# A graph network in one kernel: the build loop on TensorE rotated by half a pair, and the wide comparison on VectorE cut from 128 to 126 columns

## The reference, cut to what matters

```python
x = layernorm(x + L0(x, edges))            # h = x + segment_sum(x[src], dst); MLP; residual
x = layernorm(x + L1(x, src, dst))         # two rounds: h + mean over incoming edges, MLP, relu
x = layernorm(x + L2(x, edges, weight))    # 4 steps: neigh = segment_sum(norm * h[src], dst), tanh
x = layernorm(x + L3(x, edges, attr))      # relu(segment_sum(x[src] @ W + b + attr @ We + be, dst))
```

## Time and profile before

| | |
|---|---|
| median of 3 runs | 1121.02 us (1120.48 to 1122.2) |
| the profiled execution | 1121.91 us |
| its span, first to last instruction | 1120.1 us |
| mean granted TensorE clock | 0.977 |
| build stage on TensorE | 77.0 to 271.9 us |

### The profile page before, as it was taken

One profiled execution on the slowest core, in us unless ns is written; L12 is line 12 of the kernel. 1 busy time (PEld: TensorE's weight loads), 2 busy tenths in 40 slices (PEclk: granted clock), 3 DMA queues, 4 the chain that ended last, 5 costly groups with the idle time before them and its releaser, 6 DMA issues.

```text
span 1120.1 us, 25031 instructions
## 1 busy us (share of the span) xinstructions
PE 1027.4 (92%) x10501; PEld 626.3 (56%) x10501; DVE 520.1 (46%) x945; ACT 284.9 (25%) x584; POOL 53.9 (5%) x73
## 2 busy tenths in 40 slices
PE   0246999998999999999999999999999999999997
PEld 0245877777755555455466455564455744457455
DVE  7487999994633356322323222332222334344333
ACT  0366999997500000010000000000000001112100
POOL 4500000001000000000000000000000000000000
PEclk9966999999999999999999999999999999999999
DMA  8214778788985856877569776598774987655931
GB/s 249 74 3 174 312 315 337 321 342 330 391 368 209 336 229 244 324 295 300 200 234 408 297 294 245 178 410 325 283 265 159 393 327 306 239 199 209 411 128 33
DMA packets 55910, 299.54 MB, mean 267 GB/s; under 512 B 7264, under 2 KB 10738, under 8 KB 52403
## 3 DMA queue, kind: packets, MB, share of 16 engines
q1 hardware_dynamic: 50352, 288.14, 66.5%
q0 software_dynamic: 3344, 9.67, 2.6%
q10 hardware_dynamic: 2160, 0.98, 0.4%
HBM read 235.93 MB, written 62.86 MB: 267 GB/s over the span
## 4 chain that ended last, share of the span: by engine, by line
PE 85%; ACT 6%; issue 4%; DVE 2%; DMA 2%; PEld 0%; ACTq 0%; SPq 0%; DVEq 0%; PEldq 0%
PE ps L1367 47%; PE ps L1360 18%; PE ps L1446 6%; PE ps L1470 5%; PE ps L1322 4%; PE ps L1277 2%; ACT arena L1102 2%; ACT arena L1103 2%; PE ps L1335 2%; DMA x_buf<-in_x 1%; PE ps L1209 1%; PE ps L1304 1%; ACT arena L1044 0%; PE ps L1266 0%; DMA arena<-in_dst_blocks,win_ati 0%
## 5 line engine op out<-in xcount | busy, mean ns | idle before, releaser
L1367 PE MATMUL ps<-arena 125*128 125x500 f32 (+2 forms) x700 | 267.5, 537 | 0.0
L1367 PE MATMUL ps<-arena,parts_even 125*128 125x500 f32 (+2 forms) x700 | 267.5, 537 | 0.0
L1367 PEld LDWEIGHTS ps<-arena,parts_even 125*128 125x128 f32 x700 | 129.4, 188 | 120.6 <-issue 106.7
L1367 PEld LDWEIGHTS ps<-arena 125*128 125x128 f32 x700 | 129.3, 188 | 120.5 <-issue 106.7
L1081 ACT ACTIVATE XT<-ps 128x500 f32<-128x500 f32 (+2 forms) x49 | 26.5, 540 | 491.9 <-PE ps L1335 491.9
L1360 PE MATMUL ps<-arena 125*128 125x500 f16 (+3 forms) x700 | 139.0, 352 | 1.6 <-DVE arena L761 1.3
L1102 ACT ACTIVATE arena<-ps 128x450 f16<-128x450 f32 (+1 forms) x187 | 119.4, 639 | 23.5 <-PE ps L1470 23.5
L1470 PE MATMUL ps<-arena 64*128 64x52 f16 (+1 forms) x6300 | 99.3, 179 | 24.4 <-issue 10.2
L1103 ACT ACTIVATE arena<-ps 128x450 f32<-128x450 f32 (+1 forms) x187 | 112.9, 604 | 0.0
L1470 PEld LDWEIGHTS ps<-arena 64*128 64x128 f16 x6300 | 89.4, 94 | 42.0 <-issue 21.2
L848 DVE TENSOR_TENSOR arena<-ps,dinv 125x512 f32<-125x512 f32 (+2 forms) x28 | 17.8, 634 | 202.6 <-PE ps L1322 202.6
(11 more groups left out here) (192 smaller groups left out, 738.9 us busy)
## 6 DMA issues: line engine op xcount, KB each, us to landing
arena<-weight_mats SPq DMA_DIRECT2D x20, 3250.0 KB, 11.1
arena<-weight_mats SPq DMA_DIRECT2D x20, 3000.0 KB, 10.6
arena<-count_mats SPq DMA_DIRECT2D x15, 3125.0 KB, 14.7
weight_mats<-arena SPq DMA_DIRECT2D x25, 1562.5 KB, 8.5
count_mats<-arena SPq DMA_DIRECT2D x25, 781.2 KB, 4.3
arena<-weight_mats SPq DMA_DIRECT2D x4, 2437.5 KB, 9.2
arena<-weight_mats SPq DMA_DIRECT2D x4, 2250.0 KB, 8.5
arena<-count_mats SPq DMA_DIRECT2D x3, 2343.8 KB, 9.5
```

Source lines behind the costliest of these rows:

```text
L1367: ins = t.matmul(o, xs[:, k, :], rhs, start=(k == 0), stop=(k == NC - 1))
```

## The change

Three edits.

TensorE's pair is cut into two chunks of code. The loop now runs over q from 0 to 12; its body is the odd chunk of pair q (units 8 to 14) and then, under a condition q < 12, the even chunk of pair q+1 (units 0 to 7). The separate code of pair 0 is gone, and so pair 0 runs with the lumps of units 8, 10 and 13, whose sums nobody takes; `agg0_done` starts one lower to make up for the signal that they raise. The waits for `parts0_ok` and `blank_ok` stand ahead of pair 0. At the first tile of each odd chunk there is one more wait for `hots_ok`, of a step that was already waited for.

VectorE's comparison for `hot_hi` writes columns 0 to 125 of each tile. Columns 126 and 127 are zeroed once by Pool, in three memsets ahead of the large one, and VectorE waits for them once (`edges_ok`) ahead of its first step.

```diff
+HI = NP + 1
             def fast():
                 pool.wait_ge(rec_ok, RECS)
+                for hot in hot_hi:
+                    ins = nc.gpsimd.memset(hot[:, :, HI:128], 0.0)
+                ins.then_inc(edges_ok, 1)
                 nc.gpsimd.memset(stg_c[0][:, 0], 0.0).then_inc(blank_ok, 1)
...
-                v.tensor_tensor(hot_hi[u][:, e, :].rearrange("p t (a j) -> p t a j", j=2), numbers(iota_hi, n, 128),
-                                code(hi_c[:, bass.ds(q, 1), t0:t0 + n, :], 128), ALU.is_equal)
+                v.tensor_tensor(hot_hi[u][:, e, 0:HI].rearrange("p t (a j) -> p t a j", j=2), numbers(iota_hi[:, 0:HI], n, HI),
+                                code(hi_c[:, bass.ds(q, 1), t0:t0 + n, :], HI), ALU.is_equal)
...
                 dve.wait_ge(iotas, 1)
+                dve.wait_ge(edges_ok, 1)
...
-                pe.sem_inc(agg0_done, 2)
+                pe.sem_inc(agg0_done, 1)
...
-                def pair(q, counts):
-                    for u in range(NO_UNITS if counts is None else 0, UNITS):
+                def chunk(q, odd):
+                    counts = (stg_all[0:NP, bass.ds((q + 1) % 2, 1), 0:STG_C // 2].bitcast(F16)
+                              .rearrange("p a (j k t) -> p (a j) k t", j=2, k=NC))
+                    for u in range(UNITS_OF[0], UNITS) if odd else range(0, UNITS_OF[0]):
...
-                            if T == STEP_AT[step] or counts is None and T == TPC:
+                            if T == STEP_AT[step] or T == TPC:
                                 pe.wait_ge(hots_ok, STEPS * q + step + 1)
...
-                pair(0, None)
                 pe.wait_ge(parts0_ok, 1)
                 pe.wait_ge(blank_ok, 1)
-                with pe.Fori(1, PAIRS) as q:
-                    pair(q, stg_all[0:NP, bass.ds((q + 1) % 2, 1), 0:STG_C // 2].bitcast(F16)
-                         .rearrange("p a (j k t) -> p (a j) k t", j=2, k=NC))
+                with pe.Fori(0, PAIRS) as q:
+                    chunk(q, 1)
+                    with pe.If(q < PAIRS - 1):
+                        chunk(q + 1, 0)
```

More of the change, by code:

```diff
@@ L314, in build_program @@
         iotas = sem("iotas")
+        edges_ok = sem("edges_ok")
         dve_chain = sem("dve_chain")
@@ L1450, in sum_counts @@
                             ins.then_inc(agg0_done, 1)
-                def pair(q, counts):
-                    for u in range(NO_UNITS if counts is None else 0, UNITS):
[L1454 to L1459, removed]
+                def chunk(q, odd):
+                    counts = (stg_all[0:NP, bass.ds((q + 1) % 2, 1), 0:STG_C // 2].bitcast(F16)
+                              .rearrange("p a (j k t) -> p (a j) k t", j=2, k=NC))
+                    for u in range(UNITS_OF[0], UNITS) if odd else range(0, UNITS_OF[0]):
+                        if u == LUMP_AT[0]:
+                            pe.wait_ge(counts_out, UNITS * q)
+                        if u in LUMP_AT:
+                            k0 = KCH * LUMP_AT.index(u)
+                            sum_counts(q - 1, counts, range(k0, k0 + KCH))
                         pe.wait_ge(weights_out, UNITS * q + u - SLOTS3 + 1 + OUT_PAD)
```

## The result

| | before | changed |
|---|---|---|
| median of 19 runs each, side by side | 1122.20 us | 1118.06 us |
| lowest and highest | 1119.77, 1123.79 | 1114.03, 1121.41 |
| profiled execution (span) | 1121.91 (1120.1) | 1114.69 (1112.9) |
| ratio, with its 95% interval | | 0.9969, 0.9957 to 0.9981 |

The changed kernel is faster by 0.31% by the ratio, some 3.5 us; the two medians lie 4.1 us apart. Its runs spread over 7.4 us, where those of before spread over 4.0, and the profiled execution is one of the quickest: it shows 7.2 us less of span. So this trace shows what the change can bring, and the median tells that most runs bring less.

A forecast was written before the change was run, and what follows sets the result against it. In the build, the TensorE and ScalarE ring, 14.17 us a pair, ends last, with VectorE's 14.14 beside it. Start -5.6, turn +4.6, comparison -0.1 sum to -1.1 us: 1119.9 from a median of 1121.02, range 1115.3 to 1124.0.

The forecast's parts named there:

- its first term: Start of the build, up to unit 3's lump of pair 2: 1.9 us lost, then 7.5 gained, 5.6 us earlier.
- its second: Loop turn now between units 7 and 8, where TensorE has no gap: 0.42 us a pair, 11 pairs, 4.6 us lost.
- The first rival: The turn is cheap, 0.1 to 0.25 us, or a clock fall drops out: -3.5 us, 1115.5 to 1117.5; chance 0.28.
- with both -5.5: Within the cheap-turn rival: cheap turn and one fall of the clock dropping out together give -5.5 us.
- the bound of 2.6: Start of the build: if the longer stop lets the clock fall, three lumps cost 1 us more each, only 2.6 gained.
- the last stop at 462: TensorE's stop for code at matmul 462, its block asked for inside pair 0's store burst: about 2.2 us, resuming about 97.9.
- one at 339 matmuls: TensorE's stop for code at matmul 339, in unit 1 before the store burst: about 1.2 us.
- the term of 0.215 us: At the turn, the added unconditional branch at the conditional's end costs TensorE 0.215 us, the median branch duration.
- VectorE's comparison, -0.1: L724 on 5292 elements, 0.045 us less each; only the build's first steps pass it on, 0.1 us gained.
- A loss of the packed rate: VectorE's comparison drops out of its packed rate: 37 x 2.8 us more, about 100 us, 1215; chance 0.01.
- code at every turn: Code is loaded at every loop turn: 12 stops of about 1.1 us, 13 us, 1132; chance 0.01.
- The dear turn: The turn between units 7 and 8 costs 0.65 us or more: 1123 to 1126; chance 0.14.

The follow-up runs named there:

- the rotated loop alone: The changed kernel with VectorE's comparison at all 128 columns and without Pool's three memsets: 1102.49 us against 1107.14 of the kernel before, ratio 0.9966.
- the condition at the head: Changed kernel, loop body now the even half of pair q under q > 0, then its odd half: 1099.20 us, ratio 0.9939 to the kernel before.
- the wide comparison: The loop with the even half under q > 0 first, VectorE's comparison at 128 columns, no memsets: 1099.31 us against 1107.47 of the kernel before, ratio 0.9928.
- the two kernels with later stores: Kernel before, all even halves' stores held until the pair is done: ratio 1.0034; or only the first store of SP's loop held: ratio 0.9982.
- The early lumps alone: The kernel before, its loop unchanged, with written-out pair 0 running the lumps of units 8, 10 and 13: 1103.91 us, ratio 0.9967 to the kernel before.
- The changed kernel with the first store late: The changed kernel with pair 0's stores held until pair 1's even half is staged: 1101.01 us, ratio 0.9944 to the kernel before.
- the one without early lumps: The changed kernel with the odd chunk's lumps run only for q > 0: 1117.82 us against 1120.67 of the kernel before, ratio 0.9976.

## Why the prediction was right, and where it wasn't

**The sum.** The forecast was 1119.9 us, the result 1118.06, inside the range and faster than its middle. Against the kernel before I had -1.1 us; measured is -3.5 by the ratio and -4.1 by the medians, and the profiled execution, against that of before, has -7.2 = -10.7 (start, the narrower comparison in it) + 3.5 (turn). The form of the sum holds; its first term was mis-sized by 5 us in this execution, its second by 1.1. With the start of the rotated loop alone, where one block waits behind the burst, the sum is -7.2 to -7.9 (30.1 against 37.3 and 38.0) + 3.5 = -3.7 to -4.4 us; the ratio of that kernel gives 3.8, its medians 4.7. The same sum for the condition at the head, 61.8 (VectorE's first step) to 91.12 = 29.4 against 37.3 to 38.0 and no turn, gives -7.9 to -8.6, and the medians -7.9, with the wide comparison -8.2. By my chances the kernel would be the same within 2.2 us (0.42) rather than faster by more (0.39); it was faster by more. The first rival's -3.5 is the measured difference by luck: its start was still -5.6 and its turn 2.2. Its "with both -5.5" doesn't follow either: with a turn of 2.2 and one fall of the clock less its terms give -4.8.

**The start, -5.6 forecast, -10.7 in the profiled execution, -7.2 to -7.9 with the rotation alone.** The reading of the stops as code loaded once, and of the long one as the burst's, was right: the two kernels with later stores bear it out. The step that failed is the one that took the clock as it has it there, 0.50, and a lump at 2.2 us. The lumps that I counted as a cost of 1.0 us are what changed the clock: they fill TensorE's waits in the first step, the clock stays at or comes back to its upper level for nearly the whole start, and the lumps of pair 1 take 1.25 us. In place of that cost the traces have a gain of 2.3. I had the clock only as a risk of getting worse (the bound of 2.6), never better. The early lumps alone gain 0.33%. The count of matmuls put the last stop at 462; it came at 460 in the rotated loop alone, with 3.3 us instead of the 2.2 forecast, and not at all in the changed kernel's trace, where its packet got through 0.8 us into the burst. So 2.9 us of the 10.7 are luck of the profiled execution. The forecast value of one resumption behind the burst was a single draw of something that varies. What stays unexplained are the ordinary stops of about 1.1 us: I forecast one at 339 matmuls, and there is none in the three traces that have the changed loop's order and the early lumps. The packet for it starts at 85.3 in the changed kernel, and the 339th matmul runs near 87.6, 2.3 us behind, so it comes just in time; why it is asked for earlier, counted in matmuls, than in the kernel before, no run here settles.

**The turn, +4.6 forecast, +3.5 measured.** The pair takes 14.48 us against 14.16, 0.32 for each of eleven. The place and the mechanism were right: it sits in the stretch without slack, and moving it back under ScalarE's wait returns it. The failed step is the term of 0.215 us for the added unconditional branch, taken from the duration of the loop's compare; measured by itself it costs nothing; the row that I took it from is of a compare. Idle time alone shows 0.24 to 0.28, up from the 0.20 of the earlier trace rows. The rest is there too when starts are compared: from the first of unit 7's 92 matmuls to the lump it is 1.57 us (152.31 to 153.88), before 1.25 (118.16 to 119.41), the whole 0.32. A matmul row is 0.07 us longer than the distance to the next one, and idle time is counted only from its end. The first rival's cheap turn, 0.1 to 0.25, came closer in its reason, that the added jump costs nothing; by size 0.32 lies in the forecast's 0.3 to 0.55.

**VectorE's comparison, -0.1.** It takes 2.91 us where it took 2.95, at the packed rate, and by itself it changes the kernel by -0.08% with an interval that holds zero. It stays so where the turn is off the chain. Pool's memsets take 0.39 us for the three, over at 71.8, and nobody waits for them:

```profile
71.40 0.39 POOL L561 MEMSET arena<- 128x84 f16 x3 [24.73 <-DVE mode L703]
```

**The rivals.** A loss of the packed rate and code at every turn did not come. On the latter the Trainium skill, "Runtime: NRT & Kernel Launch", section "Instruction fetch mechanics", has a taken branch out of the two-page window wait for a fetch. The trace of the changed kernel has 0.27 us at the first turn and no packet on the instruction queue from 113 to 273 us; what did stop TensorE is a jump over code never run, 5.18 and 5.01 us in the two kernels with the conditional at the head. So the rule holds here for the first passage, not for the turns. The dear turn (0.65 us and more) is refuted.

**The falls of the clock in the settled build** are three in both, as left in the sum, 3.4 us each. The changed kernel with the first store late had four, the one without early lumps one. What sets where they land stays open, and with it part of the spread between runs. Another part lies ahead of the build: on the third chip the first tile came at 71.70 us in one kernel's trace and at 76.82 in the other's, with no edit there that would explain it.

## What to carry to other kernels

Ahead of a stage where the granted clock is at its lower level, look at what engine time is idle there: work that is useless by itself can pay if it fills that time (3.2 us here, medians on one chip), and pricing it at the lower clock misses it. Put the turn of a loop, and any conditional, at the place of the body where the engine waits for another one anyway; the turn cost 0.32 us a pair in one place and nothing in the other. And a loop's first passage competes for the DMA engines with the stores that it triggers itself, but before a store is moved away from it, look who needs the buffer.

## What the runs showed of the hardware that was not expected

- An unconditional branch in TensorE's queue cost nothing that the runs can tell, 12 times in a build (ratio 0.9998, 0.9984 to 1.0012), and left no idle time between the matmuls around it; the trace doesn't record the branch itself.
- From the start of an instruction packet to the matmul that waited for it it took 2.2 to 2.8 us in six places. Among stores it started 0.8 us after the burst began in one trace, and 5.0 to 6.5 us in eight others.
- A jump over code that was never run stopped TensorE for 5.0 to 5.2 us (two traces), with no burst of stores on the queues, as much as the longest stop behind one, 5.07.
- Thirty matmuls with no use, spread over the first 10 us of the build, left TensorE's granted clock at 0.50 for 2.7 to 3.4 us of the first 20 in six kernels with them; in six without them it was 16.3 to 18.8.
